# Two-layer slot and latent attention network: the slots' attention run side by side, their recurrent product computed in the first layer's last steps, the last batch's norm on VectorE, and the latents' first inputs loaded one stage earlier

## The reference, cut to what matters

```
x  = x + cross_attention(layernorm(x), ctx)                # first layer, per batch
f  = layernorm(x)
alpha = top-8 softmax over 64 slots of gelu([f, mean(S)] @ w1 + b1) @ w2 + b2
si = (alpha^T f) / sum(alpha)                              # [8, 64, 512]
gi = si @ Wih.T + bih                                      # input product
gh = S @ Whh.T + bhh                                       # recurrent product, S = slot_init, same for all batches
r, z = sigmoid(i_r + h_r), sigmoid(i_z + h_z);  n = tanh(i_n + r * h_n)
S_new = (1 - z) * n + z * S
attn = softmax((S_new wq + bq)(S_new wk + bk)^T * scale)   # 64 x 64 in each batch
y = layernorm(S_new + attn @ (S_new wv + bv)) * g + b
x = x + (alpha @ (y wvp + bvp)) wo + bo                    # the sum is made in the latents stage
x = x + perceiver_attention(ctx, layernorm(x));  x = x + experts(layernorm(x))
```

## Time and profile before

| | us |
|---|---|
| median of 3 runs | 2977.99 (2976.95 to 2979.15) |
| the profiled execution | 2978.57 |
| its span, first to last instruction | 2976.8 |
| TensorE busy | 2708.4 (91%) |
| VectorE busy | 2081.7 (70%) |
| ScalarE busy | 1573.6 (53%) |
| GpSimd busy | 1542.0 (52%) |

### The profile page before, as it was taken

One profiled execution on the slowest core, in us unless ns is written; L12 is line 12 of the kernel. 1 busy time (PEld: TensorE's weight loads), 2 busy tenths in 40 slices (PEclk: granted clock), 3 DMA queues, 4 the chain that ended last, 5 costly groups with the idle time before them and its releaser, 6 DMA issues. The chain is left out here.

```text
span 2976.8 us, 43504 instructions
## 1 busy us (share of the span) xinstructions
PE 2708.4 (91%) x15650; PEld 2298.4 (77%) x15650; DVE 2081.7 (70%) x4205; ACT 1573.6 (53%) x3080; POOL 1542.0 (52%) x1155
## 2 busy tenths in 40 slices
PE   6799999978668699999999999999999999799688
PEld 5688877755424598998989989989899898677576
DVE  4677777742438577777777777777777777577656
ACT  2343443431205477777777777777777677111175
POOL 2355445330002466666666666666666666365555
PEclk9899999987776799999999999999999999899899
DMA  5211222114329523223332232333322313577475
GB/s 184 56 52 55 56 55 55 54 36 165 113 83 368 178 72 101 69 73 101 79 106 69 72 101 69 79 95 78 108 69 72 99 45 126 177 269 261 160 279 190
DMA packets 184384, 337.21 MB, mean 113 GB/s; under 512 B 52360, under 2 KB 58507, under 8 KB 177101
## 3 DMA queue, kind: packets, MB, share of 16 engines
q1 hardware_dynamic: 161937, 259.40, 29.5%
q0 software_dynamic: 11680, 45.02, 4.1%
q10 hardware_dynamic: 10560, 30.08, 2.6%
HBM read 166.39 MB, written 148.71 MB: 106 GB/s over the span
## 5 line engine op out<-in xcount | busy, mean ns | idle before, releaser
L1720 POOL TENSOR_SCALAR pa_Pr<-pa_Pr,pa_rs 128x590 f32<-128x590 f32 x512 | 902.7, 1768 | 549.7 <-DVE pa_rs L1951 549.5
L1955 DVE TENSOR_REDUCE pa_least<-pa_S 128x1 f32<-128x590 f32 x512 | 391.0, 764 | 209.4 <-PE pa_S L1785 207.1
L1907 DVE TENSOR_TENSOR pa_PTl<-pa_W,pa_PTh 128x512 fp32r<-128x512 f32 (+1 forms) x640 | 420.9, 683 | 30.2 <-ACT pa_PTh L1845 23.0
L1875 ACT ACTIVATE pa_Pr<-pa_S,pa_least 128x590 f32<-128x590 f32 x512 | 384.8, 752 | 81.7 <-DVE pa_least L1955 78.3
L1845 ACT ACTIVATE pa_PTh<-pa_W 128x512 fp32r<-128x512 f32 (+1 forms) x640 | 367.4, 596 | 83.1 <-PE pa_W L1796 63.7
L1796 PE MATMUL pa_W<-pa_ident,pa_Pr 128*128 128x128 f32 (+1 forms) x2560 | 367.0, 274 | 1.2 <-DVE pa_U L1907 0.6
L1796 PEld LDWEIGHTS pa_W<-pa_ident,pa_Pr 128*128 128x128 f32 (+1 forms) x2560 | 304.8, 142 | 25.6 <-POOL pa_Pr L1720 2.8
L1810 PE MATMUL pa_O<-pa_PTh,pa_V 128*128 128x512 f32 (+1 forms) x640 | 288.7, 451 | 18.2 <-DVE pa_PTl L1907 14.0
L1811 PE MATMUL pa_O<-pa_PTl,pa_V 128*128 128x512 f32 (+1 forms) x640 | 253.9, 397 | 0.0
L1783 PE MATMUL pa_S<-pa_U,pa_Qh 128*128 128x296 f32 (+1 forms) x1024 | 227.0, 303 | 0.2
L1785 PE MATMUL pa_S<-pa_Um,pa_Ql 128*128 128x296 f32 (+1 forms) x1024 | 223.2, 299 | 0.0
(11 more groups left out here) (469 smaller groups left out, 6786.5 us busy)
## 6 DMA issues: line engine op xcount, KB each, us to landing
xs_s<-pa_Ql SPq DMA_DIRECT2D x57, 576.0 KB
pa_Um<-pa_U SPq DMA_DIRECT2D x128, 147.5 KB
pa_Qh<-pa_Qh SPq DMA_DIRECT2D x128, 128.0 KB
o_s<-pa_O_hi SPq DMA_DIRECT2D x64, 256.0 KB, 2.0
o_s<-pa_O_lo SPq DMA_DIRECT2D x64, 256.0 KB, 2.3
Wkv_hi<-o_s SPq DMA_DIRECT2D x8, 2048.0 KB, 11.6
Wkv_lo<-o_s SPq DMA_DIRECT2D x8, 2048.0 KB, 17.1
z_s<-la_z_hi ACTq DMA_DIRECT2D x8, 1180.0 KB, 7.8
```

Of the source, the lines that this page charges most:

```text
L1720: pool.tensor_scalar(p, p, rs[:, g % 2, t:t + 1], None, ALU.mult).then_inc(*pool_s.mark("probs", n))
L1875: act.activation(Pr[g % 2][:, t, :], scored[n % 2], ACT.Exp, scale=-1.0, bias=least[:, g % 2, t:t + 1], accum_out=rs[:, g % 2, t:t + 1]).t ...
L1907: dve.tensor_tensor(out, src, f32(hi_ap), ALU.subtract).then_inc(*dve_s.mark(*name))
L1955: dve.tensor_reduce(least[:, g % 2, t:t + 1], scored[n % 2], AX, ALU.min).then_inc(*dve_s.mark("least", n))
```

## The change

1. **The recurrent product moves** from the head of the slots stage into the first layer. SP loads the initial slots and the first chunk of Whh (into the tile `xa`) in step 30, the second (into the place of `E`) in step 32, the third (into `xa` again) in step 33. TensorE computes a gate in `hidden_gates` at the start of step 32, within step 34 (after `weights_and_sums`, ahead of the transposes), and at the start of step 36. ScalarE copies each to SBUF as the first thing of its own step, and SP stores all three behind the last store of si. The slots stage loads them back (0.4 MB) and adds the bias in one VectorE operation.
2. **The last batch's `xn`** is written by VectorE, not GpSimd.
3. **The slots' attention** runs phase by phase over all four pairs: all maxima, all exponentials, all scalings, all transposes, all copies, then value products and statistics. The tiles that lay in WhhT have places of their own. The inverse root is computed per pair.
4. **Gain and bias of the slots' norm** are applied as a scale and a bias per partition in the copy after the transposes, which takes two column loads with elements of 4 bytes and removes two loads spread over the partitions and eight VectorE operations.
5. **x1 of batches 0 and 1** is loaded at the end of the slots stage, into WihT, which outlives the stage; the latents use it as their x1 tiles.

```diff
@@ build_layer0
+        gh = [valid[:, 0:C * NS], valid[:, C * NS:2 * C * NS], E_flat[:, C * D:C * D + C * NS]]
+            def hidden_weights(n):
+                sp.dma_start(Whh[n % 2], rows(a["Whh_T"])[:, :, n * D:(n + 1) * D]).then_inc(Whh_in[n % 2], 16)
             for s in steps:
                 b, c = divmod(s, C)
+                if s == G - C + 2:
+                    sp.dma_start(S0T[:, :, :], rows(a["slot_init_T"])).then_inc(S0_in, 16)
+                    sp.wait_ge(*pe_s.after("xT", B - 1, C - 1))
+                    hidden_weights(0)
+                if s == G:
+                    sp.wait_ge(*pe_s.after("PT", G - 1, HC - 1))
+                    hidden_weights(1)
+                if s == G + 1:
+                    sp.wait_ge(*pe_s.after("gh", 0))
+                    hidden_weights(2)
...
+            for n in range(3):
+                sp.wait_ge(*act_s.after("free", "gh", n))
+                sp.dma_start(gh_s[:, n * C * NS:(n + 1) * C * NS], gh[n]).then_inc(gh_out, 16)
...
-                    normalise(1, "xn", xn[(b - 1) % 2], x1, b - 1)
+                    if batch(b):
+                        normalise(1, "xn", xn[(b - 1) % 2], x1, b - 1)
...
+            def hidden_gates(n):
+                ps = claim(pe, "gh", n)
+                pe.wait_ge(S0_in, 16)
+                pe.wait_ge(Whh_in[n % 2], 16 * (n // 2 + 1))
+                for c in range(C):
+                    for k in range(C):
+                        m = pe.matmul(ps[:, c * NS:(c + 1) * NS], Whh[n % 2][:, k, c * P:(c + 1) * P], S0T[:, k, :], start=(k == 0), stop=(k == C - 1))
+                m.then_inc(*pe_s.mark("gh", n))
+                if s in (G, G + 4):
+                    hidden_gates((s - G) // 2)
                 if c == 2:
                     if batch(b - 2):
                         weights_and_sums(b - 2)
+                    if s == G + 2:
+                        hidden_gates(1)
...
+                if s in (G, G + 2, G + 4):
+                    n = (s - G) // 2
+                    act.wait_ge(*pe_s.after("gh", n))
+                    act.activation(gh[n], bank_of["gh", n][:, 0:C * NS], ACT.Copy).then_inc(*act_s.mark("free", "gh", n))
...
+                if c == 2 and b == B:
+                    dve.wait_ge(*pool_s.after("ln2", "rstd", b - 1))
+                    for t in range(NT):
+                        dve.tensor_scalar(xn[(b - 1) % 2][:, t, :], x1[:, t, :], mv[1][:, t, 0:1], rstd[1][:, t:t + 1],
+                                          ALU.subtract, ALU.mult).then_inc(*dve_s.mark("xn", b - 1, t))
@@ build_slots
-            sp.dma_start(S0T[:, :, :], rows(a["slot_init_T"])).then_inc(S0_in, 16)
-            for n in range(3):
-                sp.dma_start(WhhT[:, :, n * D:(n + 1) * D], rows(a["Whh_T"])[:, :, n * D:(n + 1) * D]).then_inc(Whh_in[n], 16)
             sp.dma_start(si[:, :, :], si_s.rearrange("(j b) s d -> (b s) j d", j=NP)).then_inc(si_in, 16)
             sp.dma_start(WihT[:, :, :], rows(a["Wih_T"])).then_inc(w_in["WihT"], 16)
+            sp.dma_start(gh[:, :, :].rearrange("p g s -> p (g s)"), gh_s).then_inc(gh_in, 16)
+            sp.dma_start(S0T[:, :, :], rows(a["slot_init_T"])).then_inc(gh_in, 16)
...
+            sp.wait_ge(cut_lo, 2 * len(parts))
+            for n in range(2):
+                sp.dma_start(stage(n), x1_s[n:n + 1].rearrange("b (t p) d -> p (b t) d", p=P)).then_inc(x1_in, 16)
...
+            for dst, name in ((g_col, "g"), (b_col, "b")):
+                act.dma_start(dst[:, :], a["L0_ffn_ln_" + name].rearrange("(c p) -> p c", p=P), allow_slow_non_contiguous=True).then_inc(g_in, 16)
...
             for c in range(C):
-                copy(("yT", c), yT[:, c, :])
+                dve.wait_ge(*pe_s.at(0, "yT", c))
+                dve.tensor_scalar(yT[:, c, :], banks["yT", c][:, :], g_col[:, c:c + 1], b_col[:, c:c + 1], ALU.mult, ALU.add)\
+                   .then_inc(*dve_s.mark("yT", c))
@@ build_latents
-                sp.dma_start(x1[m][:, :, :], one(x1_s).rearrange("b (t p) d -> p (b t) d", p=P)).then_inc(ins[m]["x1"], 16)
+                if used is None:
+                    sp.sem_inc(ins[m]["x1"], 16)
+                else:
+                    sp.dma_start(x1[m], one(x1_s).rearrange("b (t p) d -> p (b t) d", p=P)).then_inc(ins[m]["x1"], 16)
```

More of the change, by code:

```diff
@@ L313, in build_layer0 @@
         hb_ready, tau_s = sem("hb_ready"), sem("tau_s")
+        S0_in, Whh_in, gh_out = sem("S0_in"), [sem(f"Whh{n}_in") for n in range(2)], sem("gh_out")
         pe_s, act_s, dve_s, pool_s = (Marks(sem(n), orders) for n in ("products", "act", "dve", "pool"))
@@ L1117, in _ @@
                   .then_inc(*pe_s.mark("A", j))
+            for j in range(NP):
                 ps = unit("AT", j)
@@ L1296, in build_latents @@
         gain = {n: (sb(n + "g", [P, C]), sb(n + "b", [P, C])) for n in ("x", "l")}
-        x1, x2 = two("x1", [P, NT, D]), two("x2", [P, NT, D])
+        x1 = [ahead[:, :, m * D:(m + 1) * D] for m in range(2)]
+        x2 = two("x2", [P, NT, D])
         aT, vo, cx = two("aT", [NS + 1, T]), two("vo", [NS + 1, D]), two("cx", [SK, D])
```

96 lines of the change are left out of this document (43 added, 53 removed).

## The result

The changed kernel takes **2943.72 us** (median of 4 runs, 2942.3 to 2945.1), the kernel before 2978.19 beside it: ratio 0.989, 95% interval 0.9877 to 0.9903. The profiled executions are 2942.3 and 2978.57 us, their spans 2940.5 and 2976.8, so 36.3 us have gone. The forecast was 2948.1 in a range of 2940 to 2958. Faster, and in the range: 36.3 us where 29.9 were forecast. But three of its stretches are off by 2 to 6.5 us, in both directions, and that is what the experiments are about.

The account below looks back on a forecast made before the run. Stages run serially behind barriers; slots is bound by queued transfers, engine round trips and VectorE's norm. 2978.57 + 5.9 (first layer) - 13.8 (head) - 11.5 (attention) - 7.0 (norm) - 3.5 (latents) = 2948.7, median 2948.1 us; range 2940 to 2958.

Parts of the forecast that it names:

- Gate 0, +3.9: First layer, head of step 32: nothing hidden; 3.4 us of product plus 0.5 of ScalarE's copy ahead of the eviction.
- Clock after gate 0, +2.1: First layer, projections after gate 0: gate and pause probably lose TensorE's full clock, +2.1 us (bounds 0 and 4).
- Norm and gate 1, -2.7: First layer, last batch: VectorE's faster norm outweighs gate 1's 3.4 us; routing product at about 650.3, gain 2.7.
- Gate 2, +1.0: First layer, wait for the routing's second cut: 3.4 us less 2.71 idle, plus a little clock (bounds -1 and +4).
- Gates' stores, +1.6: First layer's end: three more issues on SP's queue behind the last si store delay the next stage 1.6 us.
- First layer, +5.9: Sum of first-layer terms for gates, clock, norm and stores: 5.9 us longer (likely bounds 0 and +13).
- Head, -15.9: Slots stage, first transfer to first input product: about 15.0 us in place of 30.88, without recurrent weights and product.
- Cold start of the input products, +2.1: Slots stage: input products start after TensorE idles and lose 2.1 us to the half clock.
- Rival A: Slots stage: TensorE stays at half clock in the input products, 41.4 us become 83; kernel 2987; chance 0.02.
- Attention, -11.5: Slots attention, four pairs side by side: 22.0 us in place of 33.46, gain 11.5 (bounds 9 and 12).
- rival D: Whole kernel, everything at its good end: clock survives the gates (-4), packets free (-2); 2941 us; chance 0.12.
- rival C: Slots head held by column loads: 64 4-byte packets take 10.9 us, not 2.3; kernel 2957; chance 0.08.

Follow-up runs that it names:

- the experiment: Changed kernel with the three gate stores issued in step 38, ahead of the last alphaT store: 2960.26 us, single run; unaltered changed kernel on that chip 2957.98.

## Why the prediction was right, and where its terms were off

1. **Gate 0, +3.9: measured +3.6**, for the reason given: nothing is hidden behind the gate because ScalarE's copy stands ahead of the eviction. The reordered copy shows it: with the eviction first, the stall of 2.1 us goes.
2. **Clock after gate 0, +2.1: +1.4** (projection to inverse root 18.49 before, 19.93 after). Right in kind: the first projections ran at the half clock. It does not always happen: in two of the ten traces with the same code at this place the clock stayed full, and the stretch was 18.5 again.
3. **Norm and gate 1, -2.7: -4.0.** The gate was sized well (3.4, measured 3.6). The transposes were taken at 2.8, by a row at the half clock, and take 1.92 at the full one; but the wait behind them is 2.38 instead of 1.50, so that this cancels. What is left is the gate's start. The working let it begin where the sums of the batch before ended in the old trace, 3.75 us after the start of the inverse root; it begins 2.09 after it, because these sums take 3.65 us at the full clock and took 5.20 in the kernel before, in part at the half. They take 3.65 in all twelve traces with gates, 4.65 in the one without gates.
4. **Gate 2, +1.0: -1.7** between the two executions, -1.4 against the changed kernel without gates. This is the step whose sign was wrong. I counted the gate against the 2.71 us of idle time, and nothing for what the idle time had cost: in the kernel before it dropped the clock for the logits behind it. With the gate in the pause, TensorE doesn't rest, and the logits run at the full clock. Against the kernel without gates the gate alone costs 0.6, and the logits give back 2.0 (9.46 to 7.45 us from their start to the next transposes). Against the kernel before they give back 1.6 (9.07 to 7.45), and the gate costs nothing (10.77 to 10.70 us from the routing product to the logits).
5. **Gates' stores, +1.6: +1.35**, and 1.3 by the experiment. Three times the 0.45 of the row is 1.35. Beside these, the last sums took 4.57 us in the profiled execution where they had taken 5.88, with no term in the forecast. That is luck of the execution: they are at 6.2 again in six other traces and at 6.06 in one. **First layer, +5.9: -0.6**; in four of those traces, whose first layer is the changed kernel's, it is 65.6 to 65.8 us, +1.0. So some 5 us of the error belong to the forecast and 1.6 to the trace. Taken apart by the kernel without the gates, these cost 6.5, and what else changed in this stage, the norm above all (6.5), gives 7.1.
6. **Head, -15.9: -12.1.** Of its two entrances the forecast priced one well, the weights (15.0; they let the product start at 13.97 once it waits for them alone), and the other badly: the small loads at 10.8, taken from 7.8 us of landing in a row where the queue beside them moved 2 KB rows. With 6 KB rows beside them it was 12.8. The mis-sized term is this one, by 5 us; the price of the column loads (2.3) was too high by 1.9.
7. **Cold start of the input products, +2.1: +2.2** in this trace, and +0.6 to +4.2 in the twelve that start cold (71.3 to 74.9 us); that it fits to 0.1 is luck. Rival A is out: by the clock column of after, TensorE is at 0.81 in the first ten microseconds and at 1.00 in the next ten (the stretch, PE, PEld, DVE, ACT and POOL busy with their instructions, the clock, the DMA share, GB/s):

```profile
702.00:712.00 10.00, 10.00 (x20) 4.17 (x19) 2.08 (x4) 2.43 (x3) 0.00 (x0) 0.81 0.67 247
712.00:722.00 10.00, 10.00 (x25) 4.40 (x24) 4.45 (x8) 1.68 (x4) 0.00 (x0) 1.00 0.00 0
```

8. **Attention, -11.5: -11.8**, with the exponentials 1.93 us apart (1.91 forecast), VectorE pacing by 2.65 us for each pair, and the undoing worth 12.0. **Norm, -7.0: -7.1**, as forecast, but with no run that takes it back.
9. **Product with wvp, 0: -1.9**, not foreseen, cause open (above).
10. **Latents, -3.5: -4.0**, 4.5 of it at the first product, and 3.3 to 4.1 by the undoing.

In the sum, 6.5 us more from the first layer, 1.9 from the product with wvp and 1.8 from small differences stand against 3.8 less from the head: 6.4 under the forecast in the profiled execution, 4.4 in the median. The steps that carry the saving (the queue at the head, the four pairs side by side, the norm, x1) are right in their mechanism. That the total came within 0.15% is partly luck, for the head's error and the first layer's stand against each other. Two slips in the working change nothing: gate 1 from 642.82 on ends at 646.2, not 646.0, and rival D's sum is 2942.

In the Trainium skill, "DMA: Bandwidth & Descriptors", section "Queues, rings and completion order", each DMA engine goes round between the queues that have work for it, one packet at a time. The runs agree with the turns: the same 256 KB land after 7.8 and 8.0 us beside 2 KB rows, and after 12.8 beside 6 KB rows. How many rows such a packet holds is shown by no run here. The same page's rule against last dimensions that are not contiguous, which stood behind rival C, is not wrong here but small: from 678 to 722 us ScalarE's queue moved 1920 packets with the 1024 elements of 4 bytes and 864 without them, and they cost the weights 0.4 us.

## What to carry to other kernels

Where work is moved into another engine's idle time, look at the copy that fetches its result: put it behind whatever the critical path needs from the same engine, and put the new stores ahead of the last old one. When the long transfer at the head of a stage goes, ask what the short ones beside it will wait for, and let each instruction wait only for the load that it reads. And price a pause of TensorE by what runs behind it as well: work put into it may pay for itself by the clock that it keeps. Last, look at a second trace of the same kernel before you price a part by undoing it: here the same code differs by 3.6 us up to the latents' start between its two traces, on two chips, which is more than part 1 seemed to be worth.

## What the runs showed of the hardware

- The full clock stayed through gate 2: 3.7 us for its 32 recorded products of 64 columns, and the logits behind it 0.111 us each, in all twelve traces that have it. In the kernel before, the same products ran 23 us on end at the half clock. With the pause of 2.71 us in the gate's place the logits took 0.213 each, from the tenth on in the kernel before and from the sixth on in the kernel without gates.
- How long the small loads took went with the row length of the other queue's transfers, with the same bytes in it: five loads of 0.5 to 6 KB landed 3.7 to 11.9 us after issue beside 6 KB rows, and 3.9 to 7.2 us beside 2 KB rows. The 3 MB themselves landed 1.5 us later in the short rows.
- On another chip the kernel before took 2986.3 us and not 2978.2, and the changed one 2958.0 and not 2943.7, with a spread of 10 us over five runs: in the profiled executions 11 of it in the last stretch of the experts, behind the last weights' transfer (190 us against 179), where no edit of this case reaches.
